# Turning two small tiles by a product with an identity, and loading the next x blocks ahead of the diagonal blocks

## The chip, the cores and the metric

The kernel runs on one core of a Trainium2 chip. The metric is the device time of one execution in microseconds (us), the median of a few runs. TensorE, the engine of the matrix products, is called PE in the profile, and its weight loads PEld; DVE is VectorE, ACT ScalarE, POOL GpSimd, and SP the engine that issues most DMAs.

## What is computed

Four residual stages on x of shape 32 x 64 x 1024 (32 items of 64 rows). Each item picks its own small weights by an index. Cut to its core:

```python
x = x + einsum('bct,bcd->bdt', x, W0[i0])                                # mix over the 64 rows, by item
x = x + x @ W1 + (x @ A1[i0]) @ B1[i0]                                   # rank 16, by item
x = x + x @ W2.T + 0.5 * (x @ A2[i1]) @ B2.T                             # rank 32, by item
logits = x @ Wr.T + 5 * one_hot(i2); gates = softmax over the top 2
x = x + x @ W3.T + 2 * sum_e gate_e * (x @ A3[e].T) @ B3[e].T            # 8 experts of rank 16
```

## The kernel before, in words

The three big products are linear, so the kernel first multiplies the weights with one another (the first half of the time) and then sends x through the combined matrix once. Every float32 factor is held as two parts in a rounded 4-byte format (float32r), named hi and lo, and a product is the sum of three terms (hi hi, lo hi, hi lo).

The second half goes through 16 blocks of 128 rows (two items each), in 8 pairs of blocks. A pair is one run of wide products (128 x 512 columns), written out by hand with small steps put between them. For block b those small steps are, in order:

- `narrow` (24 products of 232 columns, L1296): x times the low-rank and routing columns. ACT and DVE copy the result to the tiles xn_hi and xn_lo.
- `mixed` (L1320): the diagonal block BD of the first stage times xn.
- `h1_across` (L1326): DVE has written the tile h1c (128 x 96); PE turns it, so that rows become columns, into a PSUM bank; ACT copies the turned tile to h1T; `h1_into` (L1332) multiplies it.
- `h2_across` (L1337) and `h2_into` (L1342): the same for h2c (128 x 128).
- `gated_across` (L1347): the same for the gated tile gh (128 x 128), after the top-2 routing on DVE.
- `tile` (L1349 to L1367): the output products, four to a pair.

In the first pair the wide products are the 96 of line L1374, in eight groups of twelve. There `narrow(1)` is followed by 8 wide products, `mixed(1, 1)`, 4 and 4 wide ones, and `h1_across(1, 1)`. `narrow(2)`, which belongs to the next pair, stands at the end of the first pair.

What each engine does for the first pair is a fixed list. On DVE, `route(0)` is followed by `left_lo(1)` (the lo part of the next pair's first x block, from tile `raw`), then `xn_lo(1)`, `gates(0)`, the two steps that write h1c of block 1, the split of matrix t3, and the steps that write h2c of block 1. On ACT, the copy of h2T of block 0 is followed by `left_hi(1)` (the hi part of the same x block), an exponential, and `xn_hi(1)`. SP issues, in this order: the two loads of the B1 rows (`b1s`), then in `pair_io(0)` four small loads of diagonal blocks (`bdraw`, 64 x 64 each), then two x blocks (`raw`, 512 KB each), then the output stores as they come. Each small load is preceded by an index that SP itself reads from memory into registers. The x loads wait for s_pl to be 3, which DVE raises when it has read the previous x blocks. POOL copies the low-rank columns that belong to each item (`take`), adds two halves of the x block (`first_sum`), and makes the diagonal blocks (`diagonal`).

The identity tile `ident` is written once by POOL at the start, and is read by POOL and DVE to add identities, and by PE for the turning and for 16 warm-up transpositions.

Of the kernel before, what the change touches and what calls it, by code (L numbers as in the profile page):

```python
# [22 lines left out]
F32R = mybir.dt.float32r  # L23
I32 = mybir.dt.int32
U32 = mybir.dt.uint32
ALU = mybir.AluOpType
ACT = mybir.ActivationFunctionType

P = 128
# [6 lines left out]
def cond_resid_kernel(nc, x, idx_adapter, idx_labeler, idx_language, w0, w1, a1, w2, a2, b2, w3, b3, out):  # L36
# [16 lines left out]
    SEG1 = 3 * R1  # L53
    SEG2 = 4 * R2
# [11 lines left out]
    def f32(ap):  # L66
        return ap.bitcast(F32)
# [21 lines left out]
    def at(name, shape, dtype, offset):  # L89
        return nc.alloc_sbuf_tensor_at(name, shape, dtype, offset=offset)  # L90
# [31 lines left out]
    raw = [at(f"raw{n}", [P, K, P], F32, R0 + 4096 * n) for n in range(2)]  # L122
    bdraw = [at(f"bdraw{s}", [P, P], F32, R0 + 8192 + 512 * s) for s in range(2)]
# [5 lines left out]
    def small(name, shape, dtype=F32):  # L129
        size = 4  # L130
        for n in shape[1:]:
            size *= n
        t = at(name, shape, dtype, q[0])
        q[0] += -(-size // 32) * 32
        return t

    ident = small("ident", [P, P])
    idx_a = small("idx_a", [1, B], I32)
    idx_l = small("idx_l", [1, B], I32)
    iota = small("iota", [P, E])  # L140
# [20 lines left out]
    h1c = small("h1c", [P, 2 * SEG1], F32R)  # L161
    gh = small("gh", [P, E, R3])
    h2c = small("h2c", [P, 4, R2], F32R)
# [29 lines left out]
    with ExitStack() as ctx:  # L193
        bank = [ctx.enter_context(nc.psum_tensor(f"bank{n}", [P, BANK], F32)) for n in range(8)]

        def sem(name):
            return ctx.enter_context(nc.semaphore(name))
# [12 lines left out]
        s_raw = [sem(f"s_raw{n}") for n in range(2)]  # L210
        s_id = sem("s_id")
        s_cst = sem("s_cst")
        s_diag = sem("s_diag")
        s_diag1 = sem("s_diag1")
# [25 lines left out]
        s_bdc = sem("s_bdc")  # L240
# [9 lines left out]
        s_pl = sem("s_pl")  # L250
# [19 lines left out]
        s_tg = sem("s_tg")  # L270
# [40 lines left out]
        BA, BB, BC, BD_, YB, RT = 0, 1, 2, 3, 4, 6  # L311
        Z1, Z2 = slice(SC, SC + P), slice(SC + P, SC + 2 * P)
# [17 lines left out]
        def g_block(n):  # L330

            return ORDER[n // K], n % K
# [16 lines left out]
        def _(sp):  # L349
# [65 lines left out]
            def load_w0(b, s):  # L415
                for h in range(PER):
                    a = index(idx_a, PER * b + h, NA)
                    sp.dma_start(bdraw[s][h * T:(h + 1) * T, h * T:(h + 1) * T],
                                 w0[bass.ds(a, 1)].rearrange("a c d -> (a c) d")).then_inc(s_w0[s], 16)

            def rows_of(b):
                return [(index(idx_a, PER * b + h, NA), index(idx_l, PER * b + h, NL)) for h in range(PER)]

            def load_b1s(chosen, s):

                for h, (a, lab) in enumerate(chosen):
                    rows = slice(h * SEG1, (h + 1) * SEG1)
                    for cols, scr_cols in ((slice(0, D + C3), slice(0, D + C3)),
                                           (slice(D + C3 + h * R2, D + C3 + (h + 1) * R2), bass.ds(lab * R2 + (D + C3), R2))):
                        sp.dma_start(f32(b1s[s][rows, cols]),  # L430
                                     b1scr[bass.ds(a, 1), :, :, scr_cols].rearrange("a s r c -> (a s r) c")
                                     ).then_inc(s_b1s[s], 16)
# [14 lines left out]
            sp.wait_ge(s_b1z, 2)  # L447
            load_b1s(rows_of(1), 1)

            def pair_io(p, last):  # L450
                if not last:
                    for s in range(2):
                        sp.wait_ge(s_idx, 48)
                        sp.wait_ge(s_bd, 2 * p + s + 1)
                        load_w0(2 * p + 2 + s, s)
                    if isinstance(p, int) and p == 0:
                        sp.wait_ge(s_pl, 3)
                    else:
                        sp.wait_ge(s_sum, 4 * p)
                        sp.wait_ge(s_opl, OPS * p + (5 - OPS))  # L460
                    for s in range(2):
                        sp.dma_start(raw[s][:, :, :], x[bass.ds(2 * p + 2 + s, 1)].rearrange("a p k t -> p (a k) t")).then_inc(s_raw[s], 16)
                for n, (s, c) in enumerate(TILES):
                    sp.wait_ge(s_idx, 48)
                    if n % 2 == 0:
                        sp.wait_ge(s_ya, 2 * p + n // 2 + 1)
                    else:
                        sp.wait_ge(s_yd, 2 * p + n // 2 + 1)
                    sp.dma_start(orows[bass.ds(2 * p + s, 1)].rearrange("a t d -> (a t) d")[:, c * BANK:(c + 1) * BANK], ost[n][:, :]
                                 ).then_inc(s_st[n], 16)  # L470
                    if n % 2 and not last:
                        chosen = rows_of(2 * p + 2 + s)
                        done = held(sp, 4 * p + n + 1)
                        sp.wait_ge(s_idx, 48)
                        sp.wait_ge(s_y, done)
                        load_b1s(chosen, s)

            pair_io(0, False)
            with sp.Fori(1, NP - 1) as p:
                pair_io(p, False)  # L480
# [4 lines left out]

        @block.gpsimd
        def _(pool):
            nc.gpsimd.memset(ident[:, :], 0.0).then_inc(s_id, 1)
            pool.wait_ge(s_id, 1)
            nc.gpsimd.affine_select(out=ident[:, :], in_=ident[:, :], compare_op=ALU.not_equal, fill=1.0,  # L490
                                    base=0, pattern=[[-1, P]], channel_multiplier=1).then_inc(s_id, 1)
            pool.wait_ge(s_id, 2)

            def add_identities(items):
                for kind, n in items:
                    if kind == "w":
                        pool.wait_ge(s_win[n + 2 if n else 0], 16)
                        blk = w2raw[n][:, n * P:(n + 1) * P]
                    else:
                        c, k = g_block(n)  # L500
                        if c == ORDER[0]:
                            pool.wait_ge(s_gin[k], 16)
                        else:
                            pool.wait_ge(s_g3[2 * (n // K) - 2 + k // 4], 16)
                        blk = graw[c][:, k, (k % 3) * P:(k % 3 + 1) * P]
                    nc.gpsimd.tensor_tensor(blk, blk, ident[:, :], ALU.add).then_inc(s_diag, 1)

            def store_b2(m):

# [13 lines left out]
            def diagonal(b, s, free):  # L523

                pool.wait_ge(s_w0[s], 16 * b + 32 - 16 * s)
                nc.gpsimd.tensor_tensor(bdraw[s][:, :], bdraw[s][:, :], ident[:, :], ALU.add).then_inc(s_bdc, 1)
                there, spare = held(pool, 2 * b + 1), held(pool, free)
                pool.wait_ge(s_id, 2)
                above(pool, s_mix, spare)
                pool.wait_ge(s_bdc, there)  # L530
                nc.gpsimd.tensor_copy(BD[s][0][:, :], bdraw[s][:, :]).then_inc(s_bdc, 1)
                pool.wait_ge(s_bdc, 2 * b + 2)
                nc.gpsimd.tensor_tensor(BD[s][1][:, :], bdraw[s][:, :], f32(BD[s][0][:, :]), ALU.subtract).then_inc(s_bd, 1)
# [359 lines left out]
        def _(dve):  # L893
            V = nc.vector
# [46 lines left out]
            def identity_rows(r, u):  # L941
                dve.wait_ge(s_raw[u], 8 * r + (16 - 8 * u))
                blk = raw[u][:, bass.ds(r - LORA, 1), :].rearrange("p a n -> p (a n)")
                V.tensor_tensor(blk, blk, ident[:, :], ALU.add).then_inc(s_diag1, 1)

            def rows_lo(r, u):
                for j in range(3):
# [267 lines left out]
        def _(pe):  # L1215
# [15 lines left out]

            pe.wait_ge(s_id, 2)
            for _ in range(WARM):
                nc.tensor.transpose(bank[7][:, 0:P], ident[:, :], ident[:, :])

            c = ORDER[0]
            for k in range(K):
                for a, z in TERMS:
                    pe.wait_ge(s_g3l if z else s_g3h, k + 1)
                    for ob in range(OUTER):  # L1240
                        if ob in (0, 1, K // 2):
                            pe.wait_ge(s_w2l if a else s_w2h, w2_there(k, ob))
                        ins = nc.tensor.matmul(bank[ob][:, 0:WIDTH_A[c]], W2S[a][:, k, ob * P:(ob + 1) * P], G[c][z][:, k, 0:WIDTH_A[c]],  # L1243
                                               start=(k == 0 and (a, z) == TERMS[0]), stop=(k == K - 1 and (a, z) == TERMS[-1]),
# [78 lines left out]

            def h1_across(b, s):
                pe.wait_ge(s_h1c, 2 * b + 2)
                nc.tensor.matmul(bank[RT + s][0:2 * SEG1, Z1], f32(h1c[:, :]), ident[:, :], is_transpose=True, start=False, stop=True,  # L1326
                                 skip_group_check=True).then_inc(s_th, 1)

            def h1_into(b, s, p):
# [4 lines left out]

            def h2_across(b, s):
                pe.wait_ge(s_h2c, 2 * b + 2)
                nc.tensor.matmul(bank[RT + s][0:SEG2, Z2], f32(h2c[:, :, :]).rearrange("p m r -> p (m r)"), ident[:, :], is_transpose=True,  # L1337
                                 start=False, stop=True, skip_group_check=True).then_inc(s_th, 1)

            def h2_into(b, s):  # L1340
# [3 lines left out]

            def gated_across(b, s):
                pe.wait_ge(s_gh, b + 1)
                nc.tensor.transpose(bank[RT + s][:, Z1], gh[:, :, :].rearrange("p e r -> p (e r)"), ident[:, :]).then_inc(s_tg, 1)  # L1347

            def tile(p, n, first, last):  # L1349

# [220 lines left out]
```

## Time and profile before

| what | value |
|---|---|
| median of 3 runs | 548.06 us (547.38 to 548.61) |
| the profiled execution, its own time | 548.72 us |
| its span, first to last instruction | 546.9 us |
| PE busy | 535.2 us, 98% of the span |
| DVE, ACT, POOL busy | 252.1, 162.6, 156.9 us |
| mean granted TensorE clock | 0.997 |

The profile shows one execution; its own time is 1.8 us more than its span. In rows of instructions the first number is the start in us from the span's start, the second is the duration. Matmuls are pipelined: one of 512 columns is drawn some 0.4 us long, while the next starts 0.23 us after it. So what an instruction costs PE is read from the distance of starts, not from its duration. "[3.54 <-DVE xn_lo L897]" behind a row says that the engine stood idle for 3.54 us until that instruction had ended.

### The profile page before, as it was taken

What the parts mean: (1) busy time and instruction counts of PE and PEld (TensorE: products, weight loads), DVE (VectorE), ACT (ScalarE), POOL (GpSimd) and SP (SyncE); (2) the same over time, 40 slices, a digit from 0 to 9 for tenths busy, and PEclk for the clock granted to TensorE, in tenths of its full rate; (3) what the DMA queues carried; (4) which work ended last, traced back from release to release, by engine and by line L of the source; (5) the groups of instructions that cost most, each with busy time, mean ns of one, the idle gap of its engine ahead of it and who ended that gap; (6) DMA issues with size and microseconds to landing.
All of it is one profiled execution on the core that took longest, in us unless ns stands there. A gap on an engine that the chain in (4) does not pass through costs nothing.

```text
span 546.9 us, 9086 instructions
## 1 busy us (share of the span) xinstructions
PE 535.2 (98%) x2812; PEld 476.6 (87%) x2812; DVE 252.1 (46%) x609; ACT 162.6 (30%) x314; POOL 156.9 (29%) x247
## 2 busy tenths in 40 slices
PE   7999999999999999999979999999999999999996
PEld 6999999999999999999868788888888888888885
DVE  3841322132311111214957675674756647567463
ACT  4641312121111111115623433333323333233322
POOL 2501000000001000354651744435444344443400
PEclk9999999999999999999998999999999999999999
DMA  8803020034251111120230331323313233132312
GB/s 283 292 25 130 2 77 16 1 134 149 73 178 48 40 38 44 38 82 1 61 127 2 111 117 40 108 80 110 115 38 109 78 113 112 40 107 78 112 33 77
DMA packets 24060, 46.76 MB, mean 85 GB/s; under 512 B 7636, under 2 KB 13396, under 8 KB 23908
## 3 DMA queue, kind: packets, MB, share of 16 engines
q1 hardware_dynamic: 23844, 45.85, 25.1%
q0 software_dynamic: 192, 0.59, 0.3%
q8 instruction: 14, 0.23, 0.2%
q14 instruction: 10, 0.08, 0.0%
HBM read 33.39 MB, written 13.04 MB: 85 GB/s over the span
## 4 chain that ended last, share of the span: by engine, by line
PE 91%; SPq 2%; DMA 2%; DVE 1%; POOL 1%; issue 1%; ACT 1%; POOLq 0%; DVEq 0%; ACTq 0%
PE bank L1276 26%; PE bank L1310 25%; PE bank L1227 15%; PE bank L1296 7%; PE bank L1366 4%; PE bank L1358 4%; PE bank L1243 4%; PE bank L1374 1%; PE bank L1361 1%; PE bank L1360 1%; DMA w2raw<-in_w_dram 1%; SPq L413 1%; PE bank L1320 1%; DMA raw<-in_x_dram 1%; SPq L430 1%
## 5 line engine op out<-in xcount | busy, mean ns | idle before, releaser
L1276 PE MATMUL bank<-e_lo,w1t_hi 128*128 128x488 f32 (+2 forms) x240 | 86.9, 362 | 0.0
L1276 PE MATMUL bank<-e_hi,w1t_hi 128*128 128x488 f32 (+2 forms) x240 | 86.8, 362 | 0.0
L1276 PE MATMUL bank<-e_hi,w1t_lo 128*128 128x488 f32 (+2 forms) x240 | 86.7, 361 | 0.0
L897 DVE TENSOR_TENSOR w1t_lo<-raw,w1t_hi 128x1024 fp32r<-128x1024 f32 x18 | 25.6, 1421 | 81.1 <-ACT w1t_hi L656 60.0
L1227 PE MATMUL bank<-g_hi,w2s_hi 128*128 128x384 f32 (+1 forms) x144 | 48.3, 336 | 0.3 <-DVE e_lo L897 0.3
L1276 PEld LDWEIGHTS bank<-e_lo,w1t_hi 128*128 128x128 f32 x240 | 45.2, 188 | 3.9
L1276 PEld LDWEIGHTS bank<-e_hi,w1t_hi 128*128 128x128 f32 x240 | 45.0, 188 | 4.0
L1276 PEld LDWEIGHTS bank<-e_hi,w1t_lo 128*128 128x128 f32 x240 | 45.1, 188 | 3.9
L1227 PE MATMUL bank<-g_lo,w2s_hi 128*128 128x384 f32 (+1 forms) x144 | 48.2, 335 | 0.0
L1227 PE MATMUL bank<-g_hi,w2s_lo 128*128 128x384 f32 (+1 forms) x144 | 48.2, 335 | 0.0
L897 DVE TENSOR_TENSOR e_lo<-bank,e_hi 128x384 fp32r<-128x384 f32 (+1 forms) x24 | 13.0, 558 | 60.7 <-ACT e_hi L691 60.7
L712 ACT ACTIVATE mr_left<-bank 128x384 f32 (+3 forms) x16 | 6.2, 385 | 88.4 <-PE bank L1276 88.4
L548 POOL CAST s_hi<-tba 128x256 fp32r x32 | 12.2, 408 | 70.5 <-PE bank L1296 64.9
L691 ACT ACTIVATE e_hi<-bank 128x384 fp32r<-128x384 f32 (+1 forms) x24 | 11.3, 498 | 64.6 <-PE bank L1227 56.9
L555 POOL TENSOR_TENSOR tr<-mr_right,mr_left 128x512 f32<-128x512 f32 x4 | 5.2, 1292 | 81.2 <-DMA b1scr<-b1stage_hi 46.7
L512 POOL DMA_DIRECT2D b2scr<-b2stage x3 | 1.8, 594 | 91.1 <-DVE b2stage L897 91.1
L1227 PEld LDWEIGHTS bank<-g_hi,w2s_hi 128*128 128x128 f32 x144 | 27.0, 188 | 0.6 <-DVE e_lo L897 0.6
L1227 PEld LDWEIGHTS bank<-g_hi,w2s_lo 128*128 128x128 f32 x144 | 27.0, 188 | 0.0
L1227 PEld LDWEIGHTS bank<-g_lo,w2s_hi 128*128 128x128 f32 x144 | 27.0, 188 | 0.0
L552 POOL TENSOR_TENSOR s_lo<-tba,s_hi 128x256 fp32r<-128x256 f32 x32 | 25.0, 801 | 2.4 <-POOL s_hi L548 1.1
L1310 PE MATMUL bank<-t_hi,cs_lo 128*128 128x512 f32 x56 | 22.7, 405 | 0.0
L1310 PE MATMUL bank<-t_hi,cs_hi 128*128 128x512 f32 x56 | 22.7, 405 | 0.0
(233 smaller groups left out, 1332.3 us busy)
## 6 DMA issues: line engine op xcount, KB each, us to landing
raw<-in_x_dram SPq DMA_DIRECT2D x16, 512.0 KB, 3.4
out_dram<-ost SPq DMA_DIRECT2D x32, 256.0 KB, 2.1
b1s<-b1scr SPq DMA_DIRECT2D x32, 217.5 KB, 2.8
raw<-in_b1w_dram SPq DMA_DIRECT2D x10, 512.0 KB, 3.2
w2raw<-in_w_dram SPq DMA_DIRECT2D x7, 512.0 KB, 7.9
graw<-in_w3a3wr_dram SPq DMA_DIRECT2D x4, 768.0 KB, 8.7
graw<-in_w3a3wr_dram SPq DMA_DIRECT2D x8, 196.0 KB, 7.3
b1scr<-b1stage_hi SPq DMA_DIRECT2D x8, 192.0 KB
```

The source lines that it names most:

```text
L548: nc.gpsimd.tensor_copy(S[0][:, :, at_:at_ + n], src).then_inc(s_a1c, 1)
L552: nc.gpsimd.tensor_tensor(S[1][:, :, at_:at_ + n], src, f32(S[0][:, :, at_:at_ + n]), ALU.subtract).then_inc(s_sel, 1)
L691: nc.scalar.activation(EX[c][0][:, ob, 0:w], bank[n % 6][:, 0:w], ACT.Copy).then_inc(s_acch, 1)
L712: nc.scalar.activation(dst.rearrange("p a n -> p (a n)"), stage_bank(u, j)[:, lo_:lo_ + n], ACT.Copy).then_inc(s_ra, 1)
L897: V.tensor_tensor(dst, src, f32(hi), ALU.subtract).then_inc(signal, 1)
L1227: ins = nc.tensor.matmul(to[:, 0:w], lhs, G[c][z][:, k, 0:w], start=(k == 0 and n == 0), stop=(k == K - 1 and n == len(terms) - 1), skip_g ...
L1243: ins = nc.tensor.matmul(bank[ob][:, 0:WIDTH_A[c]], W2S[a][:, k, ob * P:(ob + 1) * P], G[c][z][:, k, 0:WIDTH_A[c]], start=(k == 0 and (a, ...
L1276: ins = nc.tensor.matmul(stage_bank(u, j)[:, 0:WIDTH[c]], W1T[u][a][:, k, :], EX[c][z][:, k, :], start=(k == 0 and (a, z) == TERMS[0]), st ...
L1296: ins = nc.tensor.matmul(bank[to][:, 0:SC], left(a, k), S[z][:, k, :], start=(k == 0 and (a, z) == TERMS[0]), stop=(k == K - 1 and (a, z) ...
L1310: ins = nc.tensor.matmul(to[:, :], left[a][:, k0 + k, :], right[z][:, k, :], start=(name in OPENS and n == 0), stop=(n == 3 * KH - 1), ski ...
L1358: ins = nc.tensor.matmul(to[:, :], BD[s][a][:, :], XM[n % 2][z], start=(a, z) == TERMS[0], stop=False, skip_group_check=True)
L1366: ins = nc.tensor.matmul(to[:, :], GHT[s][a][:, :], B3[z][:, cols], start=False, stop=(a, z) == TERMS[-1], skip_group_check=True)
```

## The change

Two edits. First, h1c and h2c are turned by an ordinary product in float32r with the identity as the moving operand, in place of an fp32 transposition (a matmul with `is_transpose=True`) with the identity. For that the identity tile is declared float32r, and its other readers see it as float32. The tile gh is turned by a transposition as before. Second, for the first pair only, the two x loads are issued ahead of the four loads of diagonal blocks.

```diff
-    ident = small("ident", [P, P])
+    ident = small("ident", [P, P], F32R)
...
+            def load_x(p):
+                for s in range(2):
+                    sp.dma_start(raw[s][:, :, :], x[bass.ds(2 * p + 2 + s, 1)].rearrange("a p k t -> p (a k) t")).then_inc(s_raw[s], 16)
+
             def pair_io(p, last):
+                first = isinstance(p, int) and p == 0
+                if first:
+                    sp.wait_ge(s_pl, 3)
+                    load_x(0)
                 if not last:
                     for s in range(2):
                         sp.wait_ge(s_idx, 48)
                         sp.wait_ge(s_bd, 2 * p + s + 1)
                         load_w0(2 * p + 2 + s, s)
-                    if isinstance(p, int) and p == 0:
-                        sp.wait_ge(s_pl, 3)
-                    else:
+                    if not first:
                         sp.wait_ge(s_sum, 4 * p)
                         sp.wait_ge(s_opl, OPS * p + (5 - OPS))
-                    for s in range(2):
-                        sp.dma_start(raw[s][:, :, :], x[bass.ds(2 * p + 2 + s, 1)].rearrange("a p k t -> p (a k) t")).then_inc(s_raw[s], 16)
+                        load_x(p)
...
-            nc.gpsimd.memset(ident[:, :], 0.0).then_inc(s_id, 1)
+            nc.gpsimd.memset(f32(ident[:, :]), 0.0).then_inc(s_id, 1)
...
-                nc.tensor.transpose(bank[7][:, 0:P], ident[:, :], ident[:, :])
+                nc.tensor.transpose(bank[7][:, 0:P], f32(ident[:, :]), f32(ident[:, :]))
...
             def h1_across(b, s):
                 pe.wait_ge(s_h1c, 2 * b + 2)
-                nc.tensor.matmul(bank[RT + s][0:2 * SEG1, Z1], f32(h1c[:, :]), ident[:, :], is_transpose=True, start=False, stop=True,
+                nc.tensor.matmul(bank[RT + s][0:2 * SEG1, Z1], h1c[:, :], ident[:, :], start=False, stop=True,
                                  skip_group_check=True).then_inc(s_th, 1)
...
             def h2_across(b, s):
                 pe.wait_ge(s_h2c, 2 * b + 2)
-                nc.tensor.matmul(bank[RT + s][0:SEG2, Z2], f32(h2c[:, :, :]).rearrange("p m r -> p (m r)"), ident[:, :], is_transpose=True,
+                nc.tensor.matmul(bank[RT + s][0:SEG2, Z2], h2c[:, :, :].rearrange("p m r -> p (m r)"), ident[:, :],
                                  start=False, stop=True, skip_group_check=True).then_inc(s_th, 1)
```

SP's list at the start of the first pair's `pair_io`, before the change. `b1s` are the B1 rows of block 1, `bdraw` the diagonal blocks of blocks 2 and 3, `raw` their x blocks, and `ost` the first finished output tile; TENSOR_LOAD reads an index.

```order
L430 DMA b1s_164<-b1scr 48x32
L413 TENSOR_LOAD idx_a [waits s_bd,s_idx]
L413 ISA x2
L418 ISA
L418 DMA bdraw_118<-in_w_dram 64x64
...
L418 DMA bdraw_119<-in_w_dram 64x64
L462 DMA raw_116<-in_x_dram 128x1024 [waits s_pl]
L462 DMA raw_117<-in_x_dram 128x1024
L469 DMA out_dram<-ost_172 128x512 [waits s_ya,s_idx]
```

The same place after the change.

```order
L430 DMA b1s_164<-b1scr 48x32
L452 DMA raw_116<-in_x_dram 128x1024 [waits s_pl]
L452 DMA raw_117<-in_x_dram 128x1024
L413 TENSOR_LOAD idx_a [waits s_bd,s_idx]
L413 ISA x2
L418 ISA
L418 DMA bdraw_118<-in_w_dram 64x64
...
L418 DMA bdraw_119<-in_w_dram 64x64
L474 DMA out_dram<-ost_172 128x512 [waits s_ya,s_idx]
```

The two x loads have moved ahead of the four index reads and the four diagonal loads; nothing else on SP has.

PE's list from `mixed(1, 1)` to `h1_across(1, 1)` in the first pair, before the change (wide products of L1374 read `b_hi`, `b_lo`; `ident,h1c` is the turning).

```order
L1374 MATMUL bank<-b_lo,cs_hi 128x512
L1320 MATMUL bank<-xn_hi,bd_hi 128x232 [waits s_xnl,s_bd]
L1320 MATMUL bank<-xn_lo,bd_hi 128x232
L1320 MATMUL bank<-xn_hi,bd_lo 128x232
...
L1374 MATMUL bank<-b_hi,ds_hi 128x512
L1326 MATMUL bank<-ident,h1c 96x128 [waits s_h1c]
L1374 MATMUL bank<-b_lo,ds_hi 128x512
```

The same place after the change.

```order
L1379 MATMUL bank<-b_lo,cs_hi 128x512
L1325 MATMUL bank<-xn_hi,bd_hi 128x232 [waits s_xnl,s_bd]
L1325 MATMUL bank<-xn_lo,bd_hi 128x232
L1325 MATMUL bank<-xn_hi,bd_lo 128x232
...
L1379 MATMUL bank<-b_hi,ds_hi 128x512
L1331 MATMUL bank<-ident,h1c 96x128 [waits s_h1c]
L1379 MATMUL bank<-b_lo,ds_hi 128x512
```

Nothing has moved on PE; the turning stands in its place with the same operands, and only its kind differs (the line numbers are 5 higher).

## Rows read from the trace of the kernel before

**Rows 1.** The page's busy times: us, share of the span, instructions.

```profile
PE 535.2 (98%) x2812; PEld 476.6 (87%) x2812; DVE 252.1 (46%) x609; ACT 162.6 (30%) x314; POOL 156.9 (29%) x247
```

**Rows 2.** Waits of PE: us in total, times, longest.

```profile
PE bank L1320 <- DVE xn_lo L897: 3.5, 1, 3.5
PE bank L1347 <- DVE gh L1089: 0.8, 1, 0.8
```

**Rows 3.** Windows: stretch, length; engines' busy times (instructions); PE clock, DMA share, GB/s.

```profile
288.40:291.90 3.50, 3.50 (x11) 2.65 (x9) 3.30 (x8) 2.09 (x4) 0.00 (x0) 0.51 0.00 0
306.76:340.64 33.88, 33.88 (x181) 28.41 (x180) 20.47 (x59) 11.39 (x24) 16.36 (x29) 1.00 0.28 92
```

**Rows 4.** The chain of waits: start, length, what ran.

```profile
280.74 3.53 DMA raw<-in_x_dram
...
315.92 2.68 PE bank L1296 x24
```

**Rows 5.** Timeline of SP's DMA issues, 272 to 284 us: start, length, tiles, count.

```profile
273.63 1.99 SPq L430 DMA_DIRECT2D b1s<-b1scr  x4
276.46 4.24 SPq L418 DMA_DIRECT2D bdraw<-in_w_dram  x4
280.74 1.06 SPq L462 DMA_DIRECT2D raw<-in_x_dram  x2
```

**Rows 6.** Timeline of PE, 281 to 297 us.

```profile
281.73 0.40 PE L1374 MATMUL bank<-b_hi,cs_hi 128*128 128x512 f32 x1
...
283.34 0.39 PE L1374 MATMUL bank<-b_lo,cs_hi 128*128 128x512 f32 x1
287.26 0.34 PE L1320 MATMUL bank<-xn_hi,bd_hi 128*128 128x232 f32 x1 [3.54 <-DVE xn_lo L897]
...
296.28 0.27 PE L1296 MATMUL bank<-s_hi,w1t_hi 128*128 128x232 f32 x1
```

**Rows 7.** Timeline of ACT, 284 to 285 us.

```profile
284.29 1.06 ACT L731 ACTIVATE w1t_hi<-raw 128x1024 fp32r<-128x1024 f32 x1 [6.26 <-DMA raw<-in_x_dram]
```

**Rows 8.** Timeline of DVE, 272 to 294 us.

```profile
272.84 2.76 DVE L897 TENSOR_TENSOR t_lo<-tr,t_hi 128x2048 fp32r<-128x2048 f32 x1
...
285.38 1.42 DVE L897 TENSOR_TENSOR w1t_lo<-raw,w1t_hi 128x1024 fp32r<-128x1024 f32 x1 [5.19 <-ACT w1t_hi L731]
286.73 0.39 DVE L897 TENSOR_TENSOR xn_lo<-bank,xn_hi 128x232 fp32r<-128x232 f32 x1
...
289.36 0.38 DVE L897 TENSOR_TENSOR h1c<-bank,h1c 64x16 fp32r<-64x16 f32 x2
289.76 2.29 DVE L897 TENSOR_TENSOR t_lo<-tr,t_hi 128x2048 fp32r<-128x2048 f32 x1
292.65 0.54 DVE L1051 TENSOR_SCALAR h2c<-bank 64x96 fp32r<-64x96 f32 x2 [0.60 <-PE bank L1332]
293.23 0.41 DVE L1056 SCALAR_TENSOR_TENSOR h2c<-bank,h2c 64x32 fp32r<-64x32 f32 x2
```

**Rows 9.** Window of 277 to 278 us, columns as in Rows 3.

```profile
277.00:278.00 1.00, 1.00 (x6) 0.81 (x5) 1.00 (x1) 0.24 (x1) 0.00 (x0) 1.00 0.07 15
```

**Rows 10.** Timeline of PE in the second block pair, around three small steps.

```profile
343.28 0.39 PE L1310 MATMUL bank<-b_lo,w1t_hi 128*128 128x512 f32 x1
343.51 0.27 PE L1326 MATMUL bank<-ident,h1c 128*96 128x128 f32 x1
...
343.85 0.39 PE L1310 MATMUL bank<-t_hi,cs_hi 128*128 128x512 f32 x1
...
345.70 0.40 PE L1310 MATMUL bank<-t_hi,cs_lo 128*128 128x512 f32 x1
...
348.95 0.39 PE L1310 MATMUL bank<-t_hi,ds_hi 128*128 128x512 f32 x1
349.18 0.22 PE L1342 MATMUL bank<-b2s,h2T 128*128 128x136 f32 x1
...
349.53 0.40 PE L1310 MATMUL bank<-t_hi,ds_lo 128*128 128x512 f32 x1
```

**Rows 11.** Timeline of weight loads around the same turning of h1c.

```profile
343.28 0.12 PEld L1326 LDWEIGHTS bank<-ident,h1c 128*96 128x96 f32 x1
343.51 0.19 PEld L1310 LDWEIGHTS bank<-b_hi,w1t_lo 128*128 128x128 f32 x1
343.62 0.19 PEld L1310 LDWEIGHTS bank<-t_hi,cs_hi 128*128 128x128 f32 x1
```

More of the change, by code:

```diff
@@ L487, in _ @@
         def _(pool):
-            nc.gpsimd.memset(ident[:, :], 0.0).then_inc(s_id, 1)
+            nc.gpsimd.memset(f32(ident[:, :]), 0.0).then_inc(s_id, 1)
             pool.wait_ge(s_id, 1)
-            nc.gpsimd.affine_select(out=ident[:, :], in_=ident[:, :], compare_op=ALU.not_equal, fill=1.0,
+            nc.gpsimd.affine_select(out=ident[:, :], in_=f32(ident[:, :]), compare_op=ALU.not_equal, fill=1.0,
                                     base=0, pattern=[[-1, P]], channel_multiplier=1).then_inc(s_id, 1)
@@ L505, in add_identities @@
                         blk = graw[c][:, k, (k % 3) * P:(k % 3 + 1) * P]
-                    nc.gpsimd.tensor_tensor(blk, blk, ident[:, :], ALU.add).then_inc(s_diag, 1)
+                    nc.gpsimd.tensor_tensor(blk, blk, f32(ident[:, :]), ALU.add).then_inc(s_diag, 1)
             def store_b2(m):
@@ L525, in diagonal @@
                 pool.wait_ge(s_w0[s], 16 * b + 32 - 16 * s)
-                nc.gpsimd.tensor_tensor(bdraw[s][:, :], bdraw[s][:, :], ident[:, :], ALU.add).then_inc(s_bdc, 1)
+                nc.gpsimd.tensor_tensor(bdraw[s][:, :], bdraw[s][:, :], f32(ident[:, :]), ALU.add).then_inc(s_bdc, 1)
                 there, spare = held(pool, 2 * b + 1), held(pool, free)
@@ L943, in identity_rows @@
                 blk = raw[u][:, bass.ds(r - LORA, 1), :].rearrange("p a n -> p (a n)")
-                V.tensor_tensor(blk, blk, ident[:, :], ALU.add).then_inc(s_diag1, 1)
+                V.tensor_tensor(blk, blk, f32(ident[:, :]), ALU.add).then_inc(s_diag1, 1)
             def rows_lo(r, u):
@@ L1346, in gated_across @@
                 pe.wait_ge(s_gh, b + 1)
-                nc.tensor.transpose(bank[RT + s][:, Z1], gh[:, :, :].rearrange("p e r -> p (e r)"), ident[:, :]).then_inc(s_tg, 1)
+                nc.tensor.transpose(bank[RT + s][:, Z1], gh[:, :, :].rearrange("p e r -> p (e r)"), f32(ident[:, :])).then_inc(s_tg, 1)
             def tile(p, n, first, last):
```

## The prediction

> **What bounds the kernel now.** I read the page's busy times first: PE is busy for 535.2 us, 98% of the span, and no other engine is busy half of it [rows 1]. So time can come only from PE's few idle stretches, from PE's clock, or from cheaper work on PE. The waits of PE come next. The longest is one of 3.5 us at `mixed(1, 1)` (L1320) for DVE's xn_lo; the second, 0.8 us at the last block's gates, is far from either edit [rows 2]. The windows show a second loss right behind the long wait: from 288.4 to 291.9 us the granted clock is 0.51 with PE busy all through, which is the lower level, 1.2 GHz, after the idle stretch; a whole pair later on runs at 1.00, 2.4 GHz, without a gap [rows 3]. Last the chain of waits and the timelines, for what the long wait waits for: SP issues four diagonal loads from 276.46 to 280.70, only then the x load at 280.74; that lands 3.53 us later [rows 4, 5]. ACT has been idle for 6.26 us when it starts on it, DVE for 5.19 us when it follows with w1t_lo, and xn_lo, which has nothing to do with that x block, stands behind it in DVE's list [rows 7, 8].
>
> **The x loads, moved ahead.** SP is done with the `b1s` loads at 273.63 + 1.99 = 275.62 [rows 5]. Its wait for s_pl is for DVE's reading of the previous x blocks. In the list that comes before the t_lo split of 272.84 [rows 8], so it is over. The x loads then issue at about 275.75, 5.0 us earlier. Both are moved past four index reads and four small loads on the same queue; nothing waits for those small ones soon, since the diagonal blocks of the next pair are made only after `narrow(2)`, at 296.28 and later [rows 6]: they end about 1.1 us later, at some 281.8 (the two x issues take 1.06 [rows 5]), which costs nothing. Ahead of x in the queue are the `b1s` packets, which have drained by 277 (DMA share 0.07 from 277 to 278 [rows 9]); an x packet issued at 275.75 would hardly have moved before 276.9 anyway. So x lands between 275.75 + 3.53 = 279.3 and some 1.2 us later, 280.5.
>
> What is late next at `mixed(1, 1)`: ACT's w1t_hi takes 1.06 and DVE's w1t_lo 1.42 [rows 7, 8], so DVE comes to xn_lo at 281.8 to 283.0. xn_hi needs `narrow(1)`, which ends about where the next wide product starts, 281.73 [rows 6], plus about 0.17, plus a copy on ACT of some 0.35: 282.35. xn_lo takes 0.39 from 282.4 and PE starts about 0.14 after its end (287.12 to 287.26 before): 282.9, at worst 283.5. PE comes there one wide step of 0.23 after 283.34, at 283.57 [rows 6]. The wait goes wholly: 287.26 - 283.57 = 3.69 us.
>
> The clock: with no idle stretch I expect none of the slow one. From 287.26 to the start of `narrow(2)` at 296.28 PE took 9.02 us [rows 6]. By code that is 3 products of 232 columns, 28 wide ones and 5 small steps. At full clock a wide one costs (345.70 - 343.85) / 8 = 0.231 [rows 10], one of 232 columns 2.68 / 24 = 0.112 [rows 4], a small step 0.11 to 0.12 (below): 0.33 + 6.47 + 0.57 = 7.37. The slow clock thus cost 1.65 us; 3.5 us at 0.51 say the same, 3.5 x 0.49 = 1.7 [rows 3].
>
> Now the waits behind it. `h1_across(1, 1)` is reached at 283.57 + 0.33 + 8 x 0.231 = 285.75. DVE took 289.74 - 287.12 = 2.62 us from xn_lo's end to h1c's [rows 8]; from 282.8 that makes 285.4, plus 0.15. It fits, by 0.2 us. Then t_lo 2.29 and 1.0 for h2c give 288.7 [rows 8]; PE reaches `h2_across(1, 1)` at 285.75 + 13 x 0.231 + 3 x 0.115 = 289.1. It fits, by 0.25. Both margins are thin: DVE's t_lo took 2.76 where POOL worked beside it and 2.29 where it did not [rows 8], and `take(2)` on POOL now runs beside DVE's gates and h1c. I put 0.1 us down for it, with 0 and 1.2 us as ends (three steps stretched by 0.47, less the 0.2 of margin). Later first-pair steps have a us or so of room, and from the next pair on everything hangs on PE as before.
>
> Gain of this edit: 3.69 + 1.65 - 0.1 = 5.24, say 5.25 us.
>
> **The turning of h1c and h2c.** There are 32 of these, 2 to each of 16 blocks. In a stream at full clock one costs (343.85 - 343.28) - 2 x 0.231 = 0.11 us [rows 10]. The kernel before has no product with an identity in float32r, so I bound it. A float32r product of nearly the same size, 136 columns (L1342), costs (349.53 - 348.95) - 0.462 = 0.12 [rows 10]; one of 232 columns also 0.112 [rows 4]. So between 136 and 232 columns the count of columns does not matter. What does shows in the weight loads: the two after the turning start at 343.51 and 343.62, 0.11 apart, and never closer [rows 11]. A short instruction costs the next one's weight load, whatever it is. I take the product at 0.11, the row of 136 columns being the nearest: no change. The cheap end is by columns alone: (0.231 - 0.112) / (512 - 232) is 0.42 ns a column, so 128 columns cost 0.112 - 0.044 = 0.068, and 32 x 0.042 = 1.35 us are won. The dear end is a full wide step, 0.23, each: 32 x 0.12 = 3.8 us lost. The weight load of the turned tile gets longer, from 0.12 to the 0.19 of the float32r rows [rows 11]; it lies beside a wide product of 0.23.
>
> The Trainium skill, in Perfetto Trace Analysis, section Transposes, says that a logical transposition should be made by the transposition instruction and not by a standard matmul, because transpositions have logic that skips the arithmetic. That speaks against this edit; the rows give a short step one price whichever it is, and if the rule held here the edit would cost, up to the dear end. The skill's TensorE: Matmul & The Clock Gate, section Back-to-back issue gap, gives about 81 ns for a 128-column matmul in a stream; by it, as an estimate, 32 x 0.03 = 1 us would be won. The trace has no 128-column float32r product, and its shortest spacing for float32r is 0.11.
>
> The identity's new type costs nothing: POOL writes it once at the start, while PE still waits for the first weights, and the readers see the same bytes. ACT gets the turned tile at most some 0.05 us sooner, and nothing waits there on PE.
>
> **The sum.** 548.72 for the profiled execution, less 5.25, is 543.5. That execution stands 0.66 above the median of the runs, so I predict 548.06 - 5.25 = 542.8 us.
>
> **The rivals.**
> - The wait moves: DVE, crowded by POOL, is late with h1c or h2c of block 1, or x lands after 280.5. For it speak the margins of 0.2 us; against it, that DVE idled 5.19 us there before. Up to 1.2 us of the gain is gone: about 544.0. 15%.
> - The product is cheaper than the transposition, by its columns: 1.35 us more, 541.5. For it speaks that the turned tile has the fewest columns in the kernel; against it, the 0.11 between weight loads. 11%.
> - The product is dearer, and on the other side of zero: it doesn't overlap with its neighbours, so weight load and product stand bare, 0.19 + 0.27 [rows 10, 11] less the 0.11 of now, 0.35 each and 11.2 us in all: 548.06 + 11.2 - 5.25 = 554. It decides from 5.25 / 32 = 0.16 us each. Against it, L1342 is a float32r product in the same kind of place and overlaps. 3% for this; 3% for the milder 0.12 each, 546.6.
> - The move does nothing: x, issued earlier, lands no earlier (slower beside `b1s`), or xn_lo waits for something else: 548. Against it, the idle DVE and ACT. 3%.
>
> **How the numbers follow.** The forecast has the other 65%. The range of 8 in 10 takes the cheap-product case at its low end and the moved wait at its high end, with half a us for the spread of the runs: 541.2 to 544.4. What this kernel's measurement can tell from no change is about 0.2%, 1.1 us. Faster: 65 + 15 + 11 + 3 (the milder dear product) = 94%; the same: 3%; slower: 3%.
>
> **What would show it.** In the profile after: the x issue at about 275.7 and ACT's w1t_hi soon after 279; no wait of PE at `mixed(1, 1)`; a clock of 1.00 all through the first pair; `narrow(2)` starting near 291.0 in place of 296.28; a pair of blocks in 33.9 us as before [rows 3]; and the starts of the wide products on either side of a turning 0.57 apart. If a pair takes visibly less than 33.9, the product is cheaper; if more, dearer. A wait of PE for h1c, h2c or xn_lo in the first pair makes the first term smaller. The prediction is wrong if the slow clock stays without an idle stretch, or the pairs change.

## The result and the profile after

The kernel after takes 543.87 us (median of 8 runs, 541.86 to 546.45); the kernel before, in 8 runs beside it, 548.68 us. The ratio is 0.992, with a 95% interval of 0.9897 to 0.9942: 0.6 to 1.0% faster. The forecast was 542.8 us, a ratio of 0.990, with a range of 541.2 to 544.4. The profiled execution took 544.37 us with a span of 542.6, against 548.72 and 546.9.

The page's busy times and the waits of PE in the kernel after, beside [rows 1, 2]:

```profile
PE 533.2 (98%) x2812; PEld 476.1 (88%) x2812; DVE 252.7 (47%) x609; ACT 162.8 (30%) x314; POOL 157.1 (29%) x247
```

```profile
PE bank L1352 <- DVE gh L1094: 0.8, 1, 0.8
PE bank L1342 <- DVE h2c L1061: 0.6, 1, 0.6
```

The wait of 3.5 us at `mixed(1, 1)` is gone. The one at the last gates is as it was. A new one stands at L1342, which is `h2_across` (line numbers are 5 higher than before). PE is busy for 2 us less although its list is the same: most of that is the clock. Windows of the kernel after, beside [rows 3]:

```profile
287.30:291.90 4.60, 4.02 (x20) 2.96 (x19) 4.44 (x8) 1.90 (x4) 0.00 (x0) 1.00 0.02 4
302.67:336.50 33.83, 33.83 (x180) 28.38 (x180) 20.46 (x59) 11.40 (x24) 16.19 (x29) 1.00 0.29 93
```

The clock is 1.00 where it was 0.51. The two long windows show some 34 us at 1.00 without a gap. Their ends are set by hand and not at the same instructions, so 33.83 against 33.88 is no difference between pairs: from the start of `narrow(3)` to that of `narrow(5)` it is 34.0 us in both kernels, and the 33.9 us that the prediction gives a pair is the length of such a window. The issues of SP, beside [rows 5], and the first work on the x block, beside [rows 7]:

```profile
273.61 1.99 SPq L430 DMA_DIRECT2D b1s<-b1scr  x4
275.64 0.89 SPq L452 DMA_DIRECT2D raw<-in_x_dram  x2
277.37 4.24 SPq L418 DMA_DIRECT2D bdraw<-in_w_dram  x4
```

```profile
279.93 1.06 ACT L736 ACTIVATE w1t_hi<-raw 128x1024 fp32r<-128x1024 f32 x1 [1.93 <-DMA raw<-in_x_dram]
```

The first x load issues 5.1 us sooner, and ACT begins on it at 279.93 in place of 284.29, 4.4 us sooner. DVE in the same stretch, beside [rows 8]:

```profile
281.02 1.23 DVE L902 TENSOR_TENSOR w1t_lo<-raw,w1t_hi 128x1024 fp32r<-128x1024 f32 x1 [0.83 <-ACT w1t_hi L736]
282.33 0.40 DVE L902 TENSOR_TENSOR xn_lo<-bank,xn_hi 128x232 fp32r<-128x232 f32 x1
...
283.22 1.06 DVE L1090 TENSOR_SCALAR gm<-iota,topf,gw 128x8 f32<-128x8 f32 x2
284.31 0.65 DVE L1092 TENSOR_TENSOR gate<-gm 128x8 f32<-128x8 f32 x1
...
285.64 0.38 DVE L902 TENSOR_TENSOR h1c<-bank,h1c 64x16 fp32r<-64x16 f32 x2
286.05 3.13 DVE L902 TENSOR_TENSOR t_lo<-tr,t_hi 128x2048 fp32r<-128x2048 f32 x1
```

xn_lo ends at 282.73, in time for PE at 283.56. Behind it the gates and the t_lo split are stretched: t_lo takes 3.13 us where it took 2.29. What POOL does there:

```profile
283.49 1.45 POOL L557 TENSOR_TENSOR s_lo<-tba,s_hi 128x256 fp32r<-128x256 f32 x2
284.91 0.88 POOL L557 TENSOR_TENSOR s_lo<-a1raw,s_hi 128x128 fp32r<-128x128 f32 x2
285.75 1.28 POOL L585 TENSOR_TENSOR tmp<-raw 128x512 f32<-128x512 f32 x1
```

And PE, beside [rows 6]:

```profile
283.34 0.39 PE L1379 MATMUL bank<-b_lo,cs_hi 128*128 128x512 f32 x1
283.56 0.27 PE L1325 MATMUL bank<-xn_hi,bd_hi 128*128 128x232 f32 x1
...
285.52 0.40 PE L1379 MATMUL bank<-b_hi,ds_hi 128*128 128x512 f32 x1
286.07 0.30 PE L1331 MATMUL bank<-ident,h1c 128*96 128x128 f32 x1
...
289.27 0.40 PE L1379 MATMUL bank<-b_lo,ds_hi 128*128 128x512 f32 x1
290.25 0.33 PE L1342 MATMUL bank<-ident,h2c 128*128 128x128 f32 x1 [0.58 <-DVE h2c L1061]
...
292.20 0.26 PE L1301 MATMUL bank<-s_hi,w1t_hi 128*128 128x232 f32 x1
```

`mixed(1, 1)` starts one wide step, 0.22 us, behind its predecessor: no wait at all. `h1_across` starts 0.55 behind its own, 0.32 more than a step of 0.231, and `h2_across` 0.98, 0.75 more. A wait shorter than the drawn length of the matmul ahead (0.4 us) is not listed as idle time, or only in part, so starts tell more than the list of waits. `narrow(2)` starts at 292.20, where 291.0 was forecast and 296.28 was before.

### The profile page after: what moved, and what is told of

Read it like the earlier page. It is cut to its first block, busy times and chain, and to the rows that moved or that the text cites. A ratio compares the mean times of both kernels' runs of the same rounds, so it can differ in the third digit from the quotient of the medians.

```text
span 542.6 us, 9086 instructions
## 1 busy us (share of the span) xinstructions
PE 533.2 (98%) x2812; PEld 476.1 (88%) x2812; DVE 252.7 (47%) x609; ACT 162.8 (30%) x314; POOL 157.1 (29%) x247
## 4 chain that ended last, share of the span: by engine, by line
PE 95%; DVE 2%; DMA 1%; SPq 0%; ACT 0%; issue 0%; POOL 0%; DVEq 0%
PE bank L1281 27%; PE bank L1315 25%; PE bank L1232 15%; PE bank L1301 8%; PE bank L1363 4%; PE bank L1371 4%; PE bank L1248 4%; PE bank L1379 3%; PE bank L1366 1%; PE bank L1365 1%; DMA w2raw<-in_w_dram 1%; PE bank L1325 1%; DVE t_lo L902 1%; PE bank L1352 0%; PE bank L1337 0%; DVE gm L1090 0%
```

## The experiments

The ratios are to runs of the kernel before on the same chip. All the experiments below start from the kernel after unless it is said otherwise. Beside the time, one distance in the trace is given, because the traces differ by up to 2 us ahead of the stretch in question (`narrow(1)` starts between 277.36 and 279.43 us in them): from the start of `narrow(1)` to that of `narrow(2)`, which holds the stretch in question. It is 17.27 us before and 13.20 after, and without any wait and at full clock it would be 17.27 - 3.69 - 1.65 = 11.93. The run best, below, has a trace without a wait there: 11.94.

**Each half of the change alone**

x_only: the turning is a transposition again, for h1c as shown and for h2c likewise.

```diff
-                nc.tensor.matmul(bank[RT + s][0:2 * SEG1, Z1], h1c[:, :], ident[:, :], start=False, stop=True,
+                nc.tensor.matmul(bank[RT + s][0:2 * SEG1, Z1], f32(h1c[:, :]), f32(ident[:, :]), is_transpose=True, start=False, stop=True,
```

> The kernel after, with h1c and h2c turned by the fp32 transposition again; only the x loads are moved. Theory (the whole gain is the x loads, a turning costs 0.11 us of PE either way): the time of the kernel after, some 4.8 us under the kernel before, no PE wait at mixed(1, 1), waits of about 0.3 us for h1c and 0.7 us for h2c of block 1. Rival (the product is cheaper or dearer): the kernel after differs from this one by up to 1.3 us one way or up to 3.8 us the other, and the length of a pair of blocks by up to 0.08 or 0.24 us.

Measured: 543.91 us, ratio 0.990 (0.9886 to 0.9915), distance 13.16 us. The whole gain is there without the other half, with the same two new waits (0.2 us for h1c and 0.6 for h2c in the list). Pairs of blocks are 34.0 to 34.5 us apart in this trace, while before and order_only, with the same transpositions, have 34.0 to 34.1: a single trace can differ from another by more than the two kinds of turning do, so their price is read from the starts around one turning, at the end.

prod_only: the x loads stand behind the diagonal loads again.

```diff
-                if first:
-                    sp.wait_ge(s_pl, 3)
-                    load_x(0)
                 if not last:
...
                         load_w0(2 * p + 2 + s, s)
-                    if not first:
+                    if first:
+                        sp.wait_ge(s_pl, 3)
+                        load_x(0)
+                    else:
```

> The kernel after, with the x loads behind the diagonal loads again; only the turning is changed. Theory: the time of the kernel before within 0.3 us, the 3.5 us wait at mixed(1, 1) and the 3.5 us of clock 0.51 behind it are back. Rival (the product has a price of its own): 1.3 us faster, or up to 3.8 us slower, spread evenly over the pairs.

Measured: 548.25 us, ratio 0.9989 (0.9977 to 1.0). The distance is 18.31 us: the wait of 3.5 us is back, and the slow clock with it, for longer than in the trace of before (the window below has 0.50 throughout). How long it stays slow differs between executions of one kernel too, as told under the clock below.

```profile
288.00:292.00 4.00, 4.00 (x12) 3.08 (x11) 3.67 (x9) 1.46 (x4) 0.00 (x0) 0.50 0.00 0
```

A gain of 0.1% is not clear of none. Behind the first pair, the pairs of blocks are 33.96 to 34.03 us apart, and 34.0 to 34.03 before, but for the last (34.14).

**What made PE wait**

order_only starts from the kernel before, loads and turning unchanged. On ACT `left_hi(1)` goes behind `xn_hi(1)`, and on DVE `left_lo(1)` goes from ahead of `xn_lo(1)` to behind h2c of block 1.

```diff
-                left_hi(1)
                 exp_of(0)
                 xn_hi(1, YB)
+                left_hi(1)
...
-                left_lo(1)
                 xn_lo(1, YB)
                 gates(0, 0, steps)
...
                 second_low_rank(1, 1, steps)
+                left_lo(1)
```

> The kernel before with its late x loads and its transpositions; instead DVE and ACT take the next pair's x block later: xn_hi and xn_lo of block 1 come first, left_hi and left_lo (the parts of the x block) after them. Theory (PE waited for the x load only because xn_lo stood behind it in DVE's list): the wait at mixed(1, 1) and the slow clock vanish although x lands as late as before, 4 to 5.5 us under the kernel before. Rival (the early x transfer itself, or a different use of the queue, makes the gain): no gain, or under 1 us.

Measured: 544.64 us, ratio 0.9912 (0.9899 to 0.9926), distance 13.15 us, clock 1.00. x is issued as late as before, and the wait is gone:

```profile
281.95 0.40 DVE L897 TENSOR_TENSOR xn_lo<-bank,xn_hi 128x232 fp32r<-128x232 f32 x1 [2.14 <-ACT xn_hi L750]
```

The two new waits are there as in the kernel after: gm takes 1.03 us, t_lo 3.13, and PE waits 0.6 us for h2c. So the early x transfer is not what stretched them; the DVE steps that run earlier are.

So PE never needed the x block there. It waited because xn_lo stood behind it in two in-order lists. The same gain can be had by the order of the lists or by the order of the loads.

half_move: the x loads stand after two of the four diagonal loads.

```diff
-                if first:
-                    sp.wait_ge(s_pl, 3)
-                    load_x(0)
                 if not last:
                     for s in range(2):
+                        if first and s == 1:
+                            sp.wait_ge(s_pl, 3)
+                            load_x(0)
                         sp.wait_ge(s_idx, 48)
```

> The kernel after, with the x loads issued between the first two and the last two of the four diagonal loads: 2.1 us later than in the kernel after. Theory (chain x load, w1t_hi, w1t_lo, xn_lo; and the clock falls only behind a long idle stretch): x lands at about 281.3 us, PE waits 0.5 to 1.0 us at mixed(1, 1), the clock stays at 1.00; 3.5 to 4.5 us under the kernel before. Rival (any idle stretch there costs the clock as well): the clock falls to 0.5 for a few us, and the gain is 2 to 3 us.

Measured: 545.26 us, ratio 0.9933 (0.9919 to 0.9946), distance 14.16 us.

```profile
PE bank L1325 <- DVE xn_lo L902: 0.9, 1, 0.9
...
PE bank L1331 <- DVE h1c L902: 0.8, 1, 0.8
```

```profile
283.90:290.00 6.10, 5.27 (x25) 4.11 (x26) 5.77 (x13) 2.59 (x5) 3.35 (x5) 1.00 0.01 3
```

Two idle stretches of 0.9 and 0.8 us leave the clock at 1.00. Counted from `narrow(1)`, ACT began on x 1.9 us later than in the kernel after, and the distance grew by 1.0 us; the rest was room.

**The new waits**

pool_late: POOL waits for h1c of block 1 before `take(2)`.

```diff
+            pool.wait_ge(s_h1c, 4)
             next_blocks(0)
```

> The kernel after, with POOL held back: take(2) and first_sum start only when DVE has written h1c of block 1 (a wait on s_h1c), some 3.8 us later. Theory (POOL working beside DVE stretched DVE's gates: gm 1.06 us in place of 0.49, gate 0.65 in place of 0.17): both fall back to 0.49 and 0.17, h1c is there 1 us sooner, and the 0.3 us wait of h1_across(1, 1) is gone; the t_lo split beside POOL stays slow, so the wait for h2c shrinks or stays near 0.5 us; 0.3 to 0.8 us under the kernel after. Rival (DVE is slow for another reason): gm and gate as before.

Measured: 544.14 us, ratio 0.9913 (0.9888 to 0.9937), distance 13.10 us. DVE now runs at its own pace:

```profile
283.25 0.48 DVE L1091 TENSOR_SCALAR gm<-iota,topf,gw 128x8 f32<-128x8 f32 x2
283.77 0.17 DVE L1093 TENSOR_TENSOR gate<-gm 128x8 f32<-128x8 f32 x1
...
285.02 2.29 DVE L903 TENSOR_TENSOR t_lo<-tr,t_hi 128x2048 fp32r<-128x2048 f32 x1
```

The cause of the stretching is shown: gm fell from 1.06 to 0.48, gate from 0.65 to 0.17, t_lo from 3.13 to 2.29, and both new waits are gone. The time did not fall with them, because POOL is now late for `narrow(2)`: its last `take(2)` step ends at 292.04, and PE starts at 292.14 after an idle stretch of 1.0 us. The expectation had that rival only for the run with both edits. POOL also came later than meant: `take(2)` starts at 287.43, 5.3 us later than in the kernel after and 2.4 us after h1c is written, where 3.8 us later had been expected. By then t_lo has ended (287.31), which is why it ran at its own pace. In the run with both edits POOL's start is 2.4 us behind h1c as well, beside other DVE steps. In POOL's list the new wait stands ahead of `choose(2)`, which reads four indices into registers; that this takes the 2.4 us is likely and not shown, and the wait behind those reads was not tried.

dve_order: behind h1c of block 1 come the xm_lo copies, then h2c, then the split of t3.

```diff
-                split_lo("t3", WHOLE, SPLIT_HI["t3"])
-                second_low_rank(1, 1, steps)
                 xm_lo(0, bank[BA], 1)
                 xm_lo(1, bank[BB], 2)
+                second_low_rank(1, 1, steps)
+                split_lo("t3", WHOLE, SPLIT_HI["t3"])
```

> The kernel after, with DVE's list changed in the first pair: behind h1c of block 1 come the two xm_lo copies, then h2c, and the t3 split after it (it stood ahead of h2c). Theory (h2_across(1, 1) waits for h2c because the 3.1 us t_lo split stands ahead of it): the 0.6 us wait for h2c is gone, narrow(2) starts 0.7 us sooner, 0.7 us under the kernel after. Rival (the wait moves to xm_lo, B3 or the gates of block 1, all later by that order): no change in the start of the second pair.

Measured: 543.51 us, ratio 0.9905 (0.9881 to 0.9929), distance 12.35 us. The wait for h2c is gone, that for h1c stays. The distance is 0.85 us less, where 0.7 was expected; in the times the intervals of this kernel and of the kernel after overlap.

after_again: the kernel after once more, measured beside pool_late, dve_order and both.

> The kernel after unchanged, for comparison on the same chip as the others of this group: 4.8 us under the kernel before, with the interval of the result, 3.2 to 5.7 us.

Measured: 544.21 us, ratio 0.992 (0.9892 to 0.9947), as in the result.

both: pool_late and dve_order together.

> The kernel after with both: POOL held back until h1c of block 1 is written, and h2c ahead of the t3 split on DVE. Theory: no PE wait from mixed(1, 1) to the end of the first pair, narrow(2) starts near 291.0 us, 1.2 us under the kernel after. Rival (POOL's work is then late for narrow(2), which needs take(2)): a wait at narrow(2), and less than that.

Measured: 547.97 us, ratio 0.9985 (0.9966 to 1.0005), distance 15.56 us. The theory failed and its rival was right, by far more than thought:

```profile
287.88 2.37 DVE L903 TENSOR_TENSOR t_lo<-tr,t_hi 128x2048 fp32r<-128x2048 f32 x1
290.18 1.30 DVE L903 TENSOR_TENSOR b_lo<-b3raw,b_hi 128x1024 fp32r<-128x1024 f32 x1
```

```profile
288.06 3.58 POOL L553 CAST s_hi<-a1raw 128x128 fp32r x2
...
293.14 0.87 POOL L557 TENSOR_TENSOR s_lo<-a1raw,s_hi 128x128 fp32r<-128x128 f32 x2
```

```profile
294.11 0.53 PE L1302 MATMUL bank<-s_hi,w1t_hi 128*128 128x232 f32 x1 [3.43 <-issue]
```

```profile
294.50:297.00 2.50, 2.50 (x13) 2.50 (x13) 1.23 (x3) 0.00 (x0) 0.74 (x1) 0.50 0.00 0
```

Two casts that take POOL 0.53 us took 3.58: they ended at 291.64, just after DVE's two splits at 291.48. `narrow(2)` had to wait for POOL's last step, which ended at 294.01; PE was idle for 3.43 us (the row names no releaser), and again the clock stood at 0.50 behind a wait of that length. Nearly the whole gain was given back.

best: dve_order, and in the last pair the gates of the last block ahead of the second xm_lo copy on DVE.

```diff
-                xm_lo(1, bank[BD_], 4 * p + 2)
+                if not last:
+                    xm_lo(1, bank[BD_], 4 * p + 2)
                 gates(b1, 1, steps)
+                if last:
+                    xm_lo(1, bank[BD_], 4 * p + 2)
```

> The kernel after with h2c ahead of the t3 split on DVE in the first pair, and in the last pair the gates of the last block ahead of the second xm_lo copy on DVE. Theory: the 0.6 us wait for h2c is gone and the 0.8 us wait of the last gated_across shrinks to about 0.2 us, together 1.3 us under the kernel after, some 542.6 us where the kernel before is at 548.6. Rival (the last gates wait for ACT's exponential and not for the copy ahead of them): the last wait stays at 0.8 us, only 0.7 us is won. Second rival (the moved copy is then late for the second output product of the last pair): a new wait there of up to 0.6 us.

Measured: 542.21 us, ratio 0.9884 (0.9865 to 0.9903), distance 11.94 us. The last wait has shrunk as expected, from 0.8:

```profile
PE bank L1355 <- DVE gh L1094: 0.2, 1, 0.2
```

In this trace the wait for h1c is gone as well, which the edits were not meant to do. The same list in the first pair gave 12.35 us in dve_order, where gm took 1.07 us; here it took its own 0.48:

```profile
281.57 0.48 DVE L1090 TENSOR_SCALAR gm<-iota,topf,gw 128x8 f32<-128x8 f32 x2
```

POOL's next step starts at 281.88 here, 0.31 us after gm, and 0.28 after it in dve_order: a few hundredths of a us decided who went first, so the last 0.4 us on the way down to 11.94 is luck of this execution. best has the lowest time of all. It is faster than the kernel before; its interval still touches that of the kernel after (0.9897 to 0.9942), and the two were not measured side by side.

**What a turning costs**

dup_product and dup_transposition issue each turning of h1c and h2c four times in a row, in the kernel after and in x_only.

```diff
                 pe.wait_ge(s_h1c, 2 * b + 2)
+                (the product, or the transposition, three times more, with no signal)
```

The same stands in `h2_across`.

> The kernel after with each turning of h1c and h2c issued four times in a row into the same place (they add up, so the low-rank terms of the first two adapters are four times too large): 96 more float32r products of 128 columns. Theory (a short product costs the 0.11 us of its weight load): starts 0.11 us apart, 96 x 0.11 = 10.6 us over the kernel after. Rival (it costs its columns): starts 0.07 us apart, 6.5 us.

> The same with the fp32 transposition (x loads early as in the kernel after): 96 more transpositions, the written values being those of one or four of them. Theory: 0.11 us apart, 10.6 us over, like the product. Rival (the transposition is dearer and the single one hid it): wider apart, 0.13 us or more, over 12 us.

Starts of the four for h1c and of the wide product behind them, first as products, then as transpositions:

```profile
355.85 0.22 PE L1331 MATMUL bank<-ident,h1c 128*96 128x128 f32 x1
355.90 0.25 PE L1333 MATMUL bank<-ident,h1c 128*96 128x128 f32 x1
355.99 0.25 PE L1335 MATMUL bank<-ident,h1c 128*96 128x128 f32 x1
356.07 0.25 PE L1337 MATMUL bank<-ident,h1c 128*96 128x128 f32 x1
356.16 0.44 PE L1315 MATMUL bank<-t_hi,cs_hi 128*128 128x512 f32 x1
```

```profile
356.25 0.27 PE L1331 MATMUL bank<-ident,h1c 128*96 128x128 f32 x1
356.36 0.27 PE L1333 MATMUL bank<-ident,h1c 128*96 128x128 f32 x1
356.47 0.27 PE L1335 MATMUL bank<-ident,h1c 128*96 128x128 f32 x1
356.58 0.27 PE L1337 MATMUL bank<-ident,h1c 128*96 128x128 f32 x1
356.61 0.47 PE L1315 MATMUL bank<-t_hi,cs_hi 128*128 128x512 f32 x1
```

A product of h1c costs 0.085 us in a row and a transposition 0.11; both turnings of h2c, with 128 weight columns, stand 0.11 apart in a row. In the whole, pairs of blocks are 35.2 us apart with the products and 35.36 with the transpositions, against 34.0: 0.10 and 0.11 us for each of 12 extra turnings a pair. The single executions took 552.92 and 554.29 us, 9.0 and 10.4 over the median of the kernel after, where 10.6 had been expected for each. For h2c the 0.11 was right. For h1c as a product the two sizes seen suggest that the price follows the columns of the weights (96 against 128), since the moved columns are 128 in both; the expectation did not have that. The 0.07 by moved columns was the price of neither.

## Why the prediction was right, and where it was not

- **The cause of the wait** was right. x_only has all of the gain, half_move follows the chain x load, w1t, xn_lo, and order_only shows that xn_lo only stood behind the x block.
- **The x load**: forecast to issue at 275.75 and to land from 279.3 to 280.5; it issued at 275.64 and ACT began at 279.93. `mixed(1, 1)` was forecast at 283.57 without a wait and came at 283.56.
- **The clock**: forecast to give back 1.65 us. The windows after show 1.00. In the traces, prod_only and both, with waits of 3.5 and 3.4 us, have the slow clock; half_move, order_only and the kernel after, with waits under 1 us, have not. So the slow clock of the trace goes with the long wait. Its length is not fixed. Of 42 executions of the kernel before, 19 had a mean granted clock of 0.994 (median 549.42 us), 16 one of 0.997 as the profiled one (median 548.39 us), and 5 one of 0.999 or 1.0 (median 546.72 us). With the same code, and so presumably the same wait, the slow clock cost by these medians some 2.7 us, 1.7 us or next to nothing. The 1.65 us is the price in one execution. Two of 14 executions of the kernel after had 0.996 and took 546.4 us; where their clock fell, no trace shows.
- **The new waits** are the step that failed. The prediction put 0.1 us down; the distance has 13.20 - 11.93 = 1.27 us, 0.32 and 0.75 in the two starts, and the rest in the wide products right behind them: from the start of a turning to that of the second wide product it takes 0.43 and 0.44 us behind the two waits (286.07 to 286.50, 290.25 to 290.69), and 0.34 elsewhere. It had seen the margins of 0.2 us, knew from one row that POOL stretches DVE, and yet priced the stretching at next to nothing in the likeliest case. DVE's steps from xn_lo to h1c had shared only part of their time with POOL before; moved 4.4 us ahead they fell on `take(2)`. The 2.62 us that the prediction carried over for them held one stretched step already, which took 0.16 us after. It is this one of the kernel before, which ended at 287.96 with POOL's addition (287.94):

```profile
287.41 0.55 DVE L1082 TENSOR_TENSOR gw<-gw,ex 128x1 f32<-128x1 f32 x1
```

  In the kernel after the same way takes 3.29 us: gm and gate 1.05 more, gw 0.39 less. pool_late shows the cause. This is the first rival, put at 544.0 us and 15%; it is what happened, at 543.87, and the range held because it had been drawn to take that rival in. It should have been the forecast.
- **The turning**: forecast at no change. In place, between two wide products, its price is 0.11 us before and 0.12 after, as seen here in the kernel after beside [rows 10]. The weight loads behind the turning start 0.11 apart in both, beside [rows 11]:

```profile
339.33 0.40 PE L1315 MATMUL bank<-b_lo,w1t_hi 128*128 128x512 f32 x1
339.57 0.22 PE L1331 MATMUL bank<-ident,h1c 128*96 128x128 f32 x1
339.63 0.45 PE L1315 MATMUL bank<-b_hi,w1t_lo 128*128 128x512 f32 x1
339.91 0.40 PE L1315 MATMUL bank<-t_hi,cs_hi 128*128 128x512 f32 x1
```

```profile
339.57 0.19 PEld L1315 LDWEIGHTS bank<-b_hi,w1t_lo 128*128 128x128 f32 x1
339.68 0.19 PEld L1315 LDWEIGHTS bank<-t_hi,cs_hi 128*128 128x128 f32 x1
```

  339.91 - 339.33 is 0.58 where [rows 10] and x_only have 0.57. The transposition is drawn longer (0.27 against 0.22), and no one waits for the difference. The rule of the Trainium skill that the prediction quotes (Perfetto Trace Analysis, section Transposes), that a turning should be made by the transposition instruction, is worth 0.01 us here; four in a row of h1c go against it (0.085 us for a product, 0.11 for a transposition). The prediction's "never closer" than 0.11 was too strong: in dup_product, weight loads of 96 columns start 0.08 apart, so a short instruction does not cost one weight load of 0.11 whatever it is.

The sum: 3.69 + 1.65 - 1.27 = 4.07 us from `narrow(1)` to `narrow(2)` (17.27 - 13.20), of 4.3 us in the span; the other 0.2 us lie elsewhere and were not traced further. The medians are 4.81 us apart. That the gain came out only 0.4 us under the forecast 5.25, though 1.17 us more was lost to the new waits, is not to the prediction's credit: the kernel before was at 548.68 in eight runs and not at the 548.06 of the first three, and its executions with more of the slow clock, which the trace does not hold, count in the median.

## What to carry to other kernels

When a long wait goes, compute the next waits with the durations of the company they will then have, not with those of the trace: an engine that was idle beside a busy neighbour may fall right on it. A wait in an in-order list may have nothing to do with the data of the instruction that waits; changing places in the list can be worth as much as a faster load. And to hold back one engine to free another only moves the wait if the first is needed soon.

## What the runs showed of the hardware

DVE and POOL did not slow each other in proportion; one stood still until the other's instruction had ended. In the kernel after, t_lo starts at 286.05, while POOL's addition runs until 287.03 in its usual 1.28 us. t_lo then ends 2.15 us later, nearly the 2.29 that it takes alone, and is 0.84 us longer in all. In the run with both edits it is POOL that stands for 3 us, through two DVE splits in a row. The Trainium skill, SBUF — State Buffer, section Who interferes with whom, says that these two engines share a pair of ports under an exclusive lock, held for a whole instruction, and that the order of issue decides who stands. The lengths above agree, and in the two traces of gm (0.48 us in best, 1.07 in dve_order) the order of issue did decide. In the run with both edits POOL did not get its turn between the two DVE splits either.

A float32r weight load of 96 columns let the next product start after 0.085 us, one of 128 columns after 0.11; an fp32 transposition took 0.11 with either (dup_product and dup_transposition). Idle stretches of PE of up to 1.0 us left its granted clock at 1.00 (half_move, pool_late); ones of 3.4 and 3.5 us were followed by 0.50 or 0.51 in the three traces that have one (before, prod_only, both).
